# The D·u term of a selective scan: from VectorE to a diagonal matmul on TensorE with a ScalarE copy, beside a ring of products cut from four places to two

## The reference, cut to what matters

```python
u = _silu(conv)                                     # causal convolution of 4 taps
x_dbl = jnp.einsum('bld,ed->ble', u, x_proj_w)      # gives dt_in, Bm, Cm
dt = jax.nn.softplus(jnp.einsum('blr,er->ble', dt_in, dt_proj_w) + dt_proj_b)
def step(h, t):
    h = exp(dt_t * A) * h + (dt_t * u_t) * B_t      # per channel and state
    y_t = jnp.einsum('bdn,bn->bd', h, C_t)          # sum over the 16 states
y = jnp.swapaxes(ys, 0, 1) + u * D_param            # the term that is moved
y = y * _silu(res)
return jnp.einsum('bld,od->blo', y, out_proj_w)
```

## Time and profile before

| | |
|---|---|
| median of 3 executions | 3421.45 us (3420.22 to 3425.91) |
| the profiled execution | 3423.49 us, its span 3421.4 us |
| mean granted TensorE clock over the span | 0.959 of full |
| TensorE matmul busy | 3071.1 us (90%) |
| VectorE busy | 2650.7 us (77%) |
| ScalarE busy | 2305.4 us (67%) |
| GpSimd busy | 2354.3 us (69%) |
| layer-1 scan, first product to last scan | about 1637.6 to 2598.2 us |
| one inner chunk (chunk 3) | 119.8 us (1997.58 to 2117.38) |

### The profile page before, as it was taken

One profiled execution on the slowest core, in us unless ns is written; L12 is line 12 of the kernel. 1 busy time (PEld: TensorE's weight loads), 2 busy tenths in 40 slices (PEclk: granted clock), 3 DMA queues, 4 the chain that ended last, 5 costly groups with the idle time before them and its releaser, 6 DMA issues. The chain is left out here.

```text
span 3421.4 us, 39507 instructions
## 1 busy us (share of the span) xinstructions
PE 3071.1 (90%) x11504; PEld 1686.4 (49%) x11504; DVE 2650.7 (77%) x3528; ACT 2305.4 (67%) x3491; POOL 2354.3 (69%) x1680
## 2 busy tenths in 40 slices
PE   3589999999999999998889999998975799999998
PEld 1156676666666767774333443443332333333332
DVE  5989999999999996553899999999995344455443
ACT  2467676767677676664767677667742588888887
POOL 3578898888888887772688797788873244444443
PEclk7589999999999999999899999999998899999998
DMA  2034444444444444452222222222221122222222
GB/s 95 13 96 132 123 134 124 132 127 127 127 124 135 124 125 131 143 154 67 67 71 68 73 72 70 68 74 70 67 74 47 68 99 99 105 105 104 103 102 81
DMA packets 199619, 335.38 MB, mean 98 GB/s; under 512 B 21380, under 2 KB 57381, under 8 KB 199021
## 3 DMA queue, kind: packets, MB, share of 16 engines
q1 hardware_dynamic: 199404, 332.86, 31.8%
HBM read 325.69 MB, written 7.09 MB: 97 GB/s over the span
## 5 line engine op out<-in xcount | busy, mean ns | idle before, releaser
L1449 POOL TENSOR_TENSOR c_hc<-c_h,c_c_rep 128x1024 f32<-128x1024 f32 x256 | 602.9, 2359 | 196.6 <-DVE c_h L1500 139.5
L1921 POOL TENSOR_TENSOR d_acc<-d_acc,d_prod 128x512 f32<-128x512 f32 x240 | 318.6, 1327 | 471.8 <-DVE d_prod L1989 471.1
L1500 DVE TENSOR_TENSOR_SCAN c_h<-c_decay,c_carry,c_v_ps 128x512 f32<-128x512 f32 x512 | 629.0, 1264 | 0.0
L1881 ACT ACTIVATE d_hmid<-d_up,d_b 128x1024 f32<-128x1024 f32 x512 | 539.9, 1112 | 77.4 <-PE d_up L1782 76.9
L1346 ACT ACTIVATE c_decay<-c_dt,c_a_cols 128x512 f32<-128x512 f32 x512 | 359.5, 719 | 304.1 <-DVE c_h L1500 287.4
L1192 PE MATMUL c_y_ps<-c_hc,ident 128*128 128x512 f32 x1024 | 500.4, 612 | 67.6 <-POOL c_hc L1449 57.3
L710 POOL TENSOR_TENSOR ab_inner_low<-ab_inner,ab_inner_high 128x512 fp32r<-128x512 f32 x264 | 340.9, 1291 | 212.5 <-ACT ab_inner_high L577 210.6
L566 ACT ACTIVATE ab_gate_ps<-ab_gate_ps,ab_raw_d 128x512 f32<-128x512 f32 x264 | 174.4, 661 | 416.2 <-PE ab_gate_ps L411 416.2
L1989 DVE SCALAR_TENSOR_TENSOR d_prod<-d_eo,d_b,d_w_rep 128x512 f32<-128x512 f32 x240 | 180.1, 751 | 314.5 <-PE d_eo L1792 176.3
L692 POOL TENSOR_TENSOR ab_hc<-ab_h,ab_c_rep 128x512 f32<-128x512 f32 x256 | 330.5, 1291 | 72.6 <-DVE ab_h L773 64.4
L1782 PE MATMUL d_up<-d_heads,d_w 128*128 128x512 f32 x1024 | 336.3, 435 | 16.5 <-ACT d_hmid L1881 9.4
(11 more groups left out here) (240 smaller groups left out, 6536.3 us busy)
## 6 DMA issues: line engine op xcount, KB each, us to landing
ab_raw_gu<-in_b_experts SPq DMA_DIRECT2D x264, 256.0 KB, 3.4
ab_w_rep<-ab_w_scratch SPq DMA_DIRECT2D x264, 256.0 KB, 3.6
c_c_rep<-c_c_scratch SPq DMA_DIRECT2D x256, 256.0 KB, 3.1
d_w_rep<-d_w_scratch SPq DMA_DIRECT2D x256, 256.0 KB
ab_raw_d<-in_b_experts SPq DMA_DIRECT2D x264, 129.0 KB, 2.1
ab_raw_x<-in_xT SPq DMA_DIRECT2D x32, 256.0 KB, 4.8
out<-xT SPq DMA_DIRECT2D x8, 512.0 KB, 3.4
xT<-in_xT SPq DMA_DIRECT2D x1, 3072.0 KB, 12.7
```

Source lines behind the costliest of these rows:

```text
L1449: nc.gpsimd.tensor_tensor(hc[:, q % HC], h[:, q % HR], c_rep[:, q % BC].unsqueeze(1).broadcast_to([P, PAIR, CH]), ALU.mult).then_inc(hc_re ...
L1500: nc.vector.tensor_tensor_scan(out=h[:, q % HR, m, :], data0=decay[:, i % DEC, :], data1=v_ps[m][:], initial=carry[:, i:i + 1], op0=ALU.mu ...
L1881: nc.scalar.activation(hmid[:, (2 * q + r) % HM], up_ps[r][:], ACT.Gelu, bias=b1[:, e:e + 1]).then_inc(gelu_ready, 1)
L1921: nc.gpsimd.tensor_tensor(acc[:, s, g, :], acc[:, s, g, :], prod[:, q % PR, :], ALU.add).then_inc(add_ready, 1)
```

## The change

Four diagonals `D` are made at the start. Where a sum begins, `add_states` first puts `D·u` into the two banks by matmul, with start set there. `skip` on VectorE is gone; `leave_sum` on ScalarE copies the finished sum over `u` and raises `skip_ready`, at step 21 for pair 0, at step 5 of the next chunk for pair 1. HC goes from 4 to 2.

```diff
-    DEC, HR, HC, BC, BR = 8, 4, 4, 4, 2
+    DEC, HR, HC, BC, BR = 8, 4, 2, 4, 2
...
+        skip_diag = sb("skip_diag", [P, NM, P])
...
-        CONSTS = 7
+        CONSTS = 8
...
                 if n == 0 and not (is_int(c, 0) and pair == 0):
                     pe.wait_ge(skip_ready, c * NM + pair * PAIR)
+                if n == 0:
+                    for m in range(PAIR):
+                        at = pair * PAIR + m
+                        nc.tensor.matmul(y_ps[m][:], skip_diag[:, at, :], u[:, c % 2, at, :], start=True, stop=False)
                 pe.wait_ge(hc_ready, c * NU + q + 1 + HR)
                 for m in range(PAIR):
                     done = nc.tensor.matmul(y_ps[m][:], k["ident"], hc[:, q % HC, m, :],
-                                            start=(n == 0), stop=(n == N_STATE - 1))
+                                            start=False, stop=(n == N_STATE - 1))
...
+            def leave_sum(c, s, pair):
+                act.wait_ge(y_ready, c * NU + (pair + 1) * N_STATE + HC)
+                for m in range(PAIR):
+                    nc.scalar.copy(u[:, s, pair * PAIR + m, :], y_ps[m][:]).then_inc(skip_ready, 1)
...
+                    if q == 21:
+                        leave_sum(c, s, 0)
+                    if q == 5 and not first:
+                        leave_sum(c - 1, t, 1)
...
             activate_gate(NCH - 1)
+            leave_sum(NCH - 1, 1, 1)
             square(NCH - 1)
...
-            def skip(c, s, pair):
-                dve.wait_ge(y_ready, c * NU + (pair + 1) * N_STATE + HC)
-                for m in range(PAIR):
-                    at = pair * PAIR + m
-                    nc.vector.scalar_tensor_tensor(out=u[:, s, at, :], in0=u[:, s, at, :],
-                                                   scalar=d_skip[:, at:at + 1], in1=y_ps[m][:],
-                                                   op0=ALU.mult, op1=ALU.add).then_inc(skip_ready, 1)
...
                     scan(c, q, 0)
-                    if q == 18:
-                        skip(c, s, 0)
                     if not first:
-                        if q == 2:
-                            skip(c - 1, 1 - s, 1)
                         if q == 15:
...
+            for m in range(NM):
+                done = nc.vector.tensor_scalar(skip_diag[:, m, :], k["ident"], d_skip[:, m:m + 1], None, ALU.mult)
+            done.then_inc(const_ready, 1)
...
             over_chunks(dve, NCH, chunk)
-            skip(NCH - 1, 1, 1)
             residual(NCH - 1, 0)
```

## The result

The changed kernel takes 3429.06 us (median of 19 runs, 3423.48 to 3433.4), the kernel before, run beside it, 3424.41 (19 runs, 3420.22 to 3428.87). The profiled execution took 3428.22 us, with a span of 3426.4 (before: 3423.49 and 3421.4) at a granted clock of 0.962 (0.959).

The account below looks back on a forecast made before the run. In inner chunks TensorE was taken to set the pace up to step 15, though VectorE was full too. Terms 0 + 0.4 + 9.0 - 2.6 - 0.35 = +6.5 us on 3421.45 gave 3428.0 us, range 3414 to 3436.

Parts of the forecast that it names:

- Same: Whole kernel: time within about 0.2%, 6.8 us, of the kernel before; chance 0.44, with faster at 0.13.
- A diagonal pair takes 1.72 us: TensorE: two 512-column fp32 matmuls cost 1.72 us start to start; a rival at 0.86 us, about 3416, had chance 0.14.
- The first saving is lost whole and the matmul added: Inner chunks, steps 2 to 15: VectorE's 1.33 us saving gains nothing; step 18's product comes 1.87 us late.
- 0.15 us for leave_x: Inner chunks, step 2: ScalarE's two copies ahead of leave_x delay TensorE by 0.15 us (0 to 0.5).
- Step 18: a wait of 0.6 for the spread of step 20: Inner chunks: TensorE's added 1.72 us makes VectorE's step 20 product wait 0.6 us; then 1.2 us late.
- Mean and centre: a wait of 0.3 us, so that 1.50 remain: Inner chunks, steps 22 to 23: TensorE 3.59 us late, less 0.36 and 1.73 in hand, leaves +1.50 us a chunk.
- Chunk 0: +0.4: First chunk: no skip to save at step 2, but matmuls added; +1.72 - 1.33 = +0.4 us (0.3 to 0.9).
- Chunk 7: -2.6: Last chunk: TensorE has no next chunk to project, so both savings count; -2.6 us (-2.6 to -1.5).
- tail: -0.35: Behind the scans: skip's 1.41 us gives way to two copies of about 1.05; -0.35 us (-0.4 to 0).
- start: 0: Start: making four more diagonals holds VectorE 0.8 us, hidden while TensorE is busy; 0 (0 to 0.2).
- The ring of two: GpSimd's products with two places (HC) wait for the add two steps earlier: cost 0; rival of GpSimd held back, 3442, chance 0.13.
- Full relief: Rival: VectorE's occupancy counts, so 15 skips x 1.33 = 20 us go inside the scans; 3401.1 us, chance 0.10.

Follow-up runs that it names:

- the late error: Changed kernel with GpSimd's add_error for pair 1 moved from step 30 to step 7 of the next chunk: 3427.28 us, ratio 1.0011.

## Why the prediction was right

The forecast was 3428.0 us, +6.5 on a median of three of 3421.45; measured were +4.65 by the medians and +3.12 in the scan stage of the two profiles. "Same" had 0.44 against 0.43 for "slower", and the range of 3414 to 3436 holds 3429.06. That the time itself was met within 1.1 us is luck: the base was 3.0 us too low (the median of 19 is 3424.41) and the increase 1.9 us too high.

- *A diagonal pair takes 1.72 us.* Right: 1.71 to 1.72 in the rows of after and of the doubled diagonal.
- *The first saving is lost whole and the matmul added.* Right, and the centre of it all. Each pair alone shows it: 0 for the relief at step 2 without the matmul, +1.3 for the matmul there with the relief at step 18. The product of step 15 came 56.47 us behind the chunk's first for 54.71 before, 1.76 later for the 1.87 forecast.
- *0.15 us for leave_x behind the copies.* Wrong: 0. I had the copies wait for the sum and leave_x end at 2007.9, 0.2 us ahead of the matmul behind it, and charged the loading of its weights; the leave_x of chunk 4 ended 3.58 us behind the start of the run, as forecast, and the matmul starts where it did.
- *Step 18: a wait of 0.6 for the spread of step 20.* Right in size (0.74), wrong in place. It is the residual that waits, for project_out which TensorE starts 68.98 us into the chunk for 67.22 before; by the time of step 20 VectorE has been held already and finds its spread. I had followed only the spreads on VectorE's path here; the residual reads TensorE's work too. Step 18 gets 0.48 us shorter (5.46 to 4.98), so VectorE is +1.27 behind it.
- *Mean and centre: a wait of 0.3 us, so that 1.50 remain.* There is no such wait. TensorE ends mean 0.17 us ahead of centre, in chunk 3 (the second matmul on TensorE, then centre on VectorE):

```profile
2092.52 1.02 PE L1170 MATMUL c_work_b<-c_z,avg 128*128 128x512 f32 x2
```

```profile
2093.71 1.26 DVE L1544 TENSOR_TENSOR c_zc<-c_z,c_work_b 128x512 f32<-128x512 f32 x2
```

  So the inner chunk is what step 15 lost less what step 18 gave: 1.76 - 0.48 = 1.28, **measured +1.27 for +1.50**. The mis-sized terms are TensorE's lateness at mean and its slack ahead of it. The last add before mean starts 3.45 us late (85.45 into chunk 4 for 82.00 before), for 3.59 forecast: that is leave_x. And the slack is more than the recorded idle of 0.36: before, 2.25 us lie between the starts of that add and of mean, now 1.71, and the two matmuls of mean stand 0.86 apart for 0.93, together 0.61. That leaves 2.84 us for a distance of 1.73 to centre, less than VectorE's own lateness of 1.28 and the 1.73 together. A recorded idle time is a lower bound of the slack; the starts show all of it.
- *Chunk 0: +0.4.* Measured -1.05. Step 3 lost 1.69 and step 18 gained 1.31, as forecast. But before had 1.35 us more at steps 15 and 16 that after has not: TensorE ran there at low clock in that execution (0.76 from 1692 to 1699). I had read the chunk up to step 12 and not beyond.
- *Chunk 7: -2.6; tail: -0.35; start: 0.* Measured -2.63, -0.32, +0.04. Behind the last chunk it is ScalarE's copies that stand on the path:

```profile
2611.00 1.07 ACT L1341 COPY c_u<-c_y_ps 128x512 f32<-128x512 f32 x2 [11.46 <-PE c_y_ps L1197]
```

- *The ring of two: 0.* Right within 0.1 us in inner chunks; the 0.7 us in chunk 7 of the run with the ring alone stay open.
- *Full relief.* By VectorE's occupancy the chunk should have shrunk to 117.1; without any diagonal it took 119.3. The rule of the Trainium skill, Perfetto Trace Analysis, section Identifying the Most-Contended Engine, that for Vector occupancy shows the bottleneck, is not borne out in this stretch: 119.76 of 119.80 us were busy, and 1.33 of them could go without any gain. On matmul busy time the prediction said that the trace agrees; the rows show only that records are longer than their pitch (1.88 us for 1.72). TensorE, busy 61.77 of 61.77 us, was the engine that set the pace there.

With the measured terms, and chunk 0 taken without the 1.35 us that before had at steps 15 and 16, 6 x 1.27 + 0.38 - 2.63 - 0.32 = +5.1 us; the medians differ by 4.65. The +3.12 of the two profiles is less because their unquiet chunks fell unevenly: against the quiet lengths chunks 0 to 6 are 4.2 us longer in the profile before and 2.3 in that of after, nearly all of it at low clock, and 5.1 - 4.2 + 2.3 = 3.2. The agreement is closer than the interval (2.7 to 7.5 us) lets one claim.

## What to carry to other kernels

Where two engines are both full in a stretch, busy shares don't say which one sets the pace: compare the pitch of a step where one runs free with the pitch there (3.54 and 3.67), and the shortest distance between the releaser's start and the waiter's. In this kernel work taken from the engine that followed was worth nothing there, and work added to the one that ran without a hole cost its whole length up to the next place with slack, so ask first where that engine waits anyway, and put it there. Before removing the wait that such a run starts with, look for the second wait that the run would then start from.

## What was not expected of the hardware

**Low clock at a few places, not the same in each run.** In after's chunks 2, 3 and 5 step 1 takes 4.17 to 4.30 us for 3.54; before had this in chunks 1 and 6. The window of the first part of chunk 3 in the changed kernel (columns as above), then TensorE there:

```profile
2005.90:2011.30 5.40, 5.38 (x9) 2.35 (x10) 5.04 (x6) 5.40 (x14) 5.40 (x3) 0.68 0.20 50
```

```profile
2005.92 2.80 PE L1197 MATMUL c_y_ps<-c_hc,ident 128*128 128x512 f32 x4 [2.42 <-POOL c_hc L1464]
2008.52 2.80 PE L1089 MATMUL c_work_a<-xT,c_in_w 128*128 128x512 f32 x4
...
2127.72 1.98 PE L1197 MATMUL c_y_ps<-c_hc,ident 128*128 128x512 f32 x4 [0.78 <-POOL c_hc L1464]
```

The granted clock is 0.68 of full over this stretch, so TensorE spent a part of it at 1.2 GHz and a part at 2.4, and the same four records take 2.80 us for the 1.98 at 2127.72. Ahead of it TensorE had waited 2.42 us for GpSimd, ahead of the undisturbed one 0.78. But chunk 6 of the same kernel waited 2.42 us and kept its 1.98, and so did chunk 5 with the late error (2.41): a wait of this length doesn't decide it alone, and what does stays open. It is worth 0.6 to 1.4 us a chunk where it falls into a tight place (121.69 for 121.07 in the changed kernel, 121.86 for 120.44 with the late error), as much as the change itself.

**Waits that aren't recorded.** A product that has to wait 0.1 us for the spread shows no idle time, only 1.29 us of length for 1.26 and a pitch of 3.67 for 3.54. With pair 1 alone some ten of these hid the 1.33 us of a skip.
